# A decoder layer with a long-convolution stage and a mixture of experts: tile work moved beside the convolution and between shared expert passes

## The reference

```python
x = x + attn(layernorm(x))                       # linear attention: elu+1 feature maps, 16 heads of 32
# long convolution over the feature axis, 32 heads of 8 tokens (D_MODEL = 256 tokens, L = 512 features)
kv = einsum('bhil,bhjl->bijhl', ctx, ctx)        # products of all token pairs of a head
y  = irfft(rfft(kv, 2L) * rfft(ssm_kernel, 2L))[..., :L] + kv * D
x  = x + einsum('bijhl,bhil->bjhl', y, layernorm(x))
# mixture of experts: 16 experts, groups of 4, top 2 groups, top 4 experts, and one shared expert
w, sel = route(h @ gate_weight.T)                # h = layernorm(x), sigmoid scores
x = x + sum_e w_e * (silu(h @ G_e.T) * (h @ U_e.T)) @ D_e.T + shared(h)
```

## Time and profile before

| | us |
|---|---|
| median of 3 runs | 948.46 (948.42 to 950.93) |
| the profiled execution, its time | 946.82 |
| its span, first to last instruction | 944.0 |
| TensorE busy | 881.2 (93%) |
| VectorE busy | 592.7 (63%) |
| ScalarE busy | 377.1 (40%) |
| GpSimd busy | 385.8 (41%) |
| mean granted TensorE clock | 0.953 |

### The profile page before, as it was taken

The page is one execution under the profiler, slowest core; times in us unless marked ns, Lnnn a source line. Parts: engine busy times, 40 slices in busy tenths (PEclk is TensorE's granted clock), DMA queues, the critical chain, the costliest instruction groups (busy, mean ns, idle before and its releaser), DMA issues.

```text
span 944.0 us, 14192 instructions
## 1 busy us (share of the span) xinstructions
PE 881.2 (93%) x4356; PEld 732.3 (78%) x4356; DVE 592.7 (63%) x929; ACT 377.1 (40%) x603; POOL 385.8 (41%) x387
## 2 busy tenths in 40 slices
PE   4899999999899999967999979999999999999995
PEld 4788888888777777747987757877777777777774
DVE  5656766656479999996669964535444544444541
ACT  3323322233034433333333224556555655565552
POOL 2300000001146666653313242566565656565634
PEclk9999999999999999985569999999999999999997
DMA  9400000000026543302200145788988888888857
GB/s 330 127 1 1 1 0 0 0 0 12 23 67 203 163 110 108 108 22 74 79 34 6 67 146 170 212 217 181 210 195 201 179 206 197 200 180 196 206 112 89
DMA packets 49342, 109.39 MB, mean 116 GB/s; under 512 B 8800, under 2 KB 9312, under 8 KB 49184
## 3 DMA queue, kind: packets, MB, share of 16 engines
q0 software_dynamic: 17024, 40.48, 23.5%
q1 hardware_dynamic: 32288, 68.55, 22.1%
HBM read 78.35 MB, written 30.65 MB: 115 GB/s over the span
## 4 chain that ended last, share of the span: by engine, by line
PE 36%; DVE 7%; issue 7%; ACT 2%; POOL 1%; DMA 1%; POOLq 0%; ACTq 0%; DVEq 0%
PE PS L184 10%; PE PS L186 10%; PE PS L185 9%; PE PS L1246 3%; DVE C_rounded L1463 2%; PE PS L1184 1%; DVE y_rounded L1487 1%; PE PS L1175 1%; PE PS L1193 1%; ACT hTh L1086 1%; PE PS L1192 1%; DVE wl L1482 1%; DVE Tz_rounded L1460 1%; DMA xg<-xs_d,idx 1%; POOL xg L996 0%
## 5 line engine op out<-in xcount | busy, mean ns | idle before, releaser
L1013 POOL DMA_INDIRECT out_y<-QY,idy x72 | 119.4, 1659 | 52.7 <-ACT QY L1105 36.1
L184 PE MATMUL PS<-y_rounded,wh 128*128 128x512 f32 (+1 forms) x344 | 140.4, 408 | 0.0
L186 PE MATMUL PS<-y_rounded,wl 128*128 128x512 f32 (+1 forms) x344 | 133.9, 389 | 0.0
L185 PE MATMUL PS<-y_rounded,wh 128*128 128x512 f32 (+1 forms) x344 | 133.5, 388 | 0.0
L1497 DVE TENSOR_TENSOR hTl<-hh,hTh 128x512 fp32r<-128x512 f32 (+1 forms) x39 | 26.5, 679 | 119.4 <-ACT hTh L1086 114.5
L996 POOL DMA_INDIRECT xg<-xs_d,idx x76 | 79.0, 1040 | 34.9 <-issue 17.8
L246 POOL TENSOR_SCALAR var_eps<-mean_var 128x2 f32<-128x2 f32 x15 | 3.3, 219 | 196.2 <-DVE mean_var L357 196.2
L195 PE MATMUL PS<-qER,Tz 128*128 128x288 f32 x320 | 80.8, 407 | 1.5 <-ACT QY L318 0.8
L195 PE MATMUL PS<-prod,Tz 128*128 128x288 f32 x320 | 81.9, 412 | 0.0
L1487 DVE TENSOR_TENSOR y_rounded<-PS,y_rounded 128x512 fp32r<-128x512 f32 x76 | 50.7, 687 | 42.2 <-ACT y_rounded L1098 41.4
L186 PEld LDWEIGHTS PS<-y_rounded,wl 128*128 128x128 f32 x344 | 65.0, 189 | 14.2
(11 more groups left out here) (215 smaller groups left out, 1950.2 us busy)
## 6 DMA issues: line engine op xcount, KB each, us to landing
ws<-in_gu_w SPq DMA_DIRECT2D x38, 512.0 KB
ws<-in_dn_w SPq DMA_DIRECT2D x20, 512.0 KB, 5.3
C<-in_ctx SPq DMA_DIRECT2D x32, 256.0 KB, 2.7
Tz<-kpad_d SPq DMA_DIRECT2D x32, 256.0 KB, 3.2
xs_d<-xn SPq DMA_DIRECT2D x16, 256.0 KB, 2.0
out_y<-X SPq DMA_DIRECT2D x16, 256.0 KB
X<-in_x SPq DMA_DIRECT2D x1, 3072.0 KB, 18.7
xg<-xs_d,idx POOLq DMA_INDIRECT x76
```

The lines of the kernel that those rows point to most:

```text
L184: pe.matmul(out_, lh, rh, start=first, stop=False)
L185: pe.matmul(out_, lh, rl, start=False, stop=False)
L186: return pe.matmul(out_, ll, rh, start=False, stop=last)
L1013: nc.gpsimd.indirect_dma_start(out=out, out_offset=bass.IndirectOffsetOnAxis(ap=idy[:, t:t + 1], axis=0), in_=yo[:, t], in_offset=None, co ...
```

## The change

- Tiles are taken in another order (`tile_at`): first the eight first halves of the sequences, then the second halves. Four of them (`EARLY`) go through `t3`, addition, norm, `t4` and the split during the convolution's heads 18 to 27: their transposes write into the unused PSUM columns (`in_gaps`) behind a head's convolution. `convolve` gets a `behind` argument for that. Their router passes and stores come too; the routers run right after the last head.
- GpSimd's split of the shared weights moves from the end into heads 12 to 17, in three parts.
- The shared expert's group 0 and part of group 1 run in single steps (`shared_step`, six passes of 512 columns; `down5`) between the other twelve tiles. The down passes of all groups now come before the first slot, and the last placings lie between those of group 3; `body(0)` has no down passes.
- The counts: TensorE forms, in one PSUM bank, the count of each expert within the tile and over all tiles before it, by 16 further passes with `ones_r` over `SELr`; VectorE's running totals over tiles fall away, and those over experts become one product with a lower triangle (`lower`) and a sum.
- The one-hot matrices are formed from `free_ps`, a copy of `free` in PSUM that TensorE makes.
- VectorE's `w_lo(0, 1)` and `add_shared`, and ScalarE's `w_hi(0, 1)`, change their place around the first slots.

```diff
-def convolve(pe, i, k, chunks=range(DC)):
+def convolve(pe, i, k, chunks=range(DC), behind=None):
...
+        if behind is not None and c == DC - 1:
+            mm = behind()
...
+EARLY = SLOT_T
+ODD = CD * 2
+tile_at = [TPB * b + t for t in range(TPB) for b in range(B)]
...
+def stream_head(e):
+    return CH // 2 + 2 + 2 * e
+
+def normal_head(e):
+    return CH // 2 + 5 + 2 * e
...
+def add_to_stream(dve, n):
+    i = tile_at[n]
+    if n < EARLY:
+        h = stream_head(n)
+        dve.wait_ge(conv_ps[h % 2], DC * (h // 2 + 1))
+        dve.tensor_tensor(by_gaps(X[:, i]), by_gaps(X[:, i]), in_gaps(h % 2), ALU.add).then_inc(x2_done, 1)
+    else:
+        dve.wait_ge(t3_ps, n - EARLY + 1)
+        dve.tensor_tensor(X[:, i], X[:, i], PS[:, 4 + n % 2], ALU.add).then_inc(x2_done, 1)
+    wait_apart(dve, x2_done, n + 1)
+    dve.bn_stats(bst3[n % 4][:], X[:, i]).then_inc(bn3, 1)
+    if n >= 4:
+        wait_apart(dve, nb3s, n - 3)
+    wait_apart(dve, bn3, n + 1)
+    dve.bn_aggr(mv3[n % 4][:], bst3[n % 4][:]).then_inc(mv3s, 1)
...
+def x3_low(dve, n):
+    dve.wait_ge(xT_hi, n + 1)
+    if n < EARLY:
+        dve.tensor_tensor(low_tile(n).rearrange("p c (b n) -> p c b n", n=ODD), in_gaps(normal_head(n) % 2),
+                          high_tile(n).bitcast(F32).rearrange("p c (b n) -> p c b n", n=ODD), ALU.subtract).then_inc(xT_lo, 1)
...
+        for part in range(NG - 1):
+            pair_of_heads(6 + part)
+            shared_lo(2 * part, 2 * part + 2)
+        for e in range(EARLY):
+            pair_of_heads(stream_head(e) // 2)
+            rstd3(pool, e)
+        for i in range(stream_head(EARLY) // 2, CH // 2 - 1):
+            pair_of_heads(i)
...
+        for h in range(stream_head(0), CH):
+            head(h // 2, h % 2)
+            for e in range(EARLY):
+                if h == stream_head(e) + 2:
+                    norm(act, e)
+                if h == normal_head(e):
+                    x3_high(act, e)
...
+        for h in range(stream_head(0), CH):
+            for e in range(EARLY):
+                if h == normal_head(e):
+                    dve.wait_ge(xT_hi, e + 1)
+            terms_ahead(h // 2, h % 2)
+            for e in range(EARLY):
+                if h == stream_head(e):
+                    add_to_stream(dve, e)
+                if h == normal_head(e):
+                    x3_low(dve, e)
+            reduce((h - 1) // 2, (h - 1) % 2)
+            terms_behind(h // 2, h % 2)
...
+        for h in range(stream_head(0), CH):
+            behind = None
+            for e in range(EARLY):
+                if h == stream_head(e):
+                    behind = functools.partial(stream_back, e)
+                if h == normal_head(e):
+                    behind = functools.partial(normal_across, e)
+                if h == stream_head(e) + 2:
+                    pe.wait_ge(x2_done, e + 1)
+                if h == normal_head(e) + 2:
+                    pe.wait_ge(xT_lo, e + 1)
+            convolve(pe, h // 2, h % 2, behind=behind)
...
+        rstd3(pool, 4)
+        hidden(0, 0)
+        rstd3(pool, 5)
+        hid_lo(0, 0)
+        for n in range(6, 9):
+            rstd3(pool, n)
+        wait_apart(pool, r_in, 16 * 6)
+        nc.gpsimd.tensor_copy(tri_r[:], tri[:]).then_inc(tri_done, 1)
+        rstd3(pool, 9)
+        hidden(0, 1)
+        rstd3(pool, 10)
+        rstd3(pool, 11)
+        hid_lo(0, 1)
+        for n in range(12, NT):
+            rstd3(pool, n)
+        for g in range(1, NG):
             for c in range(IC):
                 hidden(g, c)
                 hid_lo(g, c)
-        hidden(NG - 1, 0)
...
+        for n in range(EARLY, NT):
+            if n > EARLY:
+                x3_high(act, n - 1)
+            norm(act, n)
+            if n == 5:
+                hid_hi(0, 0)
+            if n == 8:
+                silu(0, 1)
+                up(0, 1)
+            if n == 10:
+                hid_hi(0, 1)
+                act.activation(table_row[:], ident[:, 0:1], ACT.Sigmoid)
+            if n > 12:
+                y_shared_out(0, n - 13)
...
+        for n in range(EARLY):
+            router(n)
+        for d in range(DC - 1):
+            shared_step(0, 0, d)
+        t3(EARLY)
+        t3(EARLY + 1)
+        shared_step(0, 0, DC - 1)
+        steps = {4: (0, 1, 0), 5: (0, 1, 1), 6: (0, 1, 2), 7: (0, 1, 3), 9: (1, 0, 0), 10: (1, 0, 1), 11: (1, 0, 2)}
+        for n in range(EARLY, NT):
+            if n + 2 < NT:
+                t3(n + 2)
+            if n in steps:
+                shared_step(*steps[n])
+            t4(n)
+            if n > 11:
+                down5(0, n - 12)
+            if n > EARLY:
+                router(n - 1)
+        shared_step(1, 0, 3)
         router(NT - 1)
 
-        shared_gate_up(0, 0)
...
+        pe.matmul(free_ps, ident[:], free[:], start=True, stop=True).then_inc(free_ready, 1)
+        shared_gate_up(1, 1)
+        shared_gate_up(2, 0)
+        shared_down(1)
         pe.wait_ge(sel_done, 1)
-        pe.wait_ge(r_in, 16 * 6)
-        pe.wait_ge(memsets, 5)
-        sel = SEL[:].rearrange("p t e -> p (t e)")
-        pe.matmul(PS[:, 4, 0:NT * NE], tri[:], sel, start=True, stop=True)
-        pe.matmul(PS[:, 4, NT * NE:], ones[:], sel, start=True, stop=True).then_inc(count_ps, 1)
-        shared_down(0)
-        shared_gate_up(1, 1)
-        shared_gate_up(2, 0, placing=0)
-        shared_down(1, placing=SLOT_T)
-        shared_gate_up(2, 1, placing=2 * SLOT_T)
-        shared_gate_up(3, 0, placing=3 * SLOT_T)
-        shared_down(2)
-        shared_gate_up(3, 1)
+        pe.wait_ge(memsets, 6)
+        pe.wait_ge(tri_done, 1)
+        pe.matmul(PS[:, 4, 0:(NT + 1) * NE], tri_r[:], SELr[:].rearrange("p t e -> p (t e)"), start=True, stop=False)
+        for t in range(NT):
+            mm = pe.matmul(PS[:, 4, (t + 1) * NE:(NT + 1) * NE].rearrange("p (t e) -> p t e", e=NE), ones_r[:],
+                           SELr[:, t].unsqueeze(1).broadcast_to([P, NT - t, NE]), start=False, stop=(t == NT - 1))
+        mm.then_inc(count_ps, 1)
+        shared_gate_up(2, 1)
+        shared_step(3, 0, 0)
+        shared_step(3, 0, 1)
+        place(0)
+        shared_step(3, 0, 2)
+        place(1)
+        shared_step(3, 0, 3)
+        place(2)
+        for t in range(SLOT_T):
+            down5(2, t)
+            place(3 + t)
+        for d in range(DC):
+            shared_step(3, 1, d)
+            place(7 + d)
+        place(11)
+        place(12)
+        place(13)
+        down5(3, 0)
+        place(14)
+        down5(3, 1)
+        place(15)
+        down5(3, 2)
+        down5(3, 3)
...
-        link(dve.tensor_copy(TOT[:].rearrange("p t e -> p (t e)"), PS[:, 4, NT * NE:]))
-        cur, k, n = TOT, 1, 0
-        while k < NT:
-            nxt = acc[n % 2]
-            post(dve.tensor_copy(nxt[:, 0:k], cur[:, 0:k]))
-            tt(nxt[:, k:], cur[:, k:], cur[:, 0:NT - k], ALU.add)
-            cur, k, n = nxt, 2 * k, n + 1
-
-        tt(NSK[:], cur[:, NT - 1].unsqueeze(2).broadcast_to([P, NE, B * S // SLOT]),
+        tt(NSK[:], PS[:, 4, NT * NE:(NT + 1) * NE].unsqueeze(2).broadcast_to([P, NE, B * S // SLOT]),
            slotk[:].unsqueeze(1).broadcast_to([P, NE, B * S // SLOT]), ALU.is_gt)
         reduce(NS[:], NSK[:])
-        tt_post(POS[:], cur[:], TOT[:], ALU.subtract)
-        cur, k, n = NS, 1, 0
-        while k < NE:
-            nxt = se[n % 2]
-            post(dve.tensor_copy(nxt[:, 0:k], cur[:, 0:k]))
-            tt(nxt[:, k:], cur[:, k:], cur[:, 0:NE - k], ALU.add)
-            cur, k, n = nxt, 2 * k, n + 1
-        ends = cur
-        tt(base[:], ends[:], NS[:], ALU.subtract)
-        link(dve.tensor_scalar(base[:], base[:], float(SLOT), None, ALU.mult))
-
-        tt(POS[:], POS[:], base[:].unsqueeze(1).broadcast_to([P, NT, NE]), ALU.add)
-        tt(POS[:].rearrange("p t e -> p (t e)"), POS[:].rearrange("p t e -> p (t e)"), PS[:, 4, 0:NT * NE], ALU.add)
+        tt(before, lower[:], NS[:].unsqueeze(1).broadcast_to([P, NE, NE]), ALU.mult)
+        reduce(base[:], before)
+        post(dve.tensor_tensor(ends[:], base[:], NS[:], ALU.add))
+        link(dve.scalar_tensor_tensor(out=POS[:], in0=base[:].unsqueeze(1).broadcast_to([P, NT, NE]), scalar=float(SLOT),
+                                      in1=PS[:, 4, 0:NT * NE].rearrange("p (t e) -> p t e", t=NT), op0=ALU.mult, op1=ALU.add))
...
+            dve.tensor_tensor(lowhot[p], free_ps.unsqueeze(1).broadcast_to([P, TOPK, P]),
...
+                dve.tensor_scalar(colhot[p][:, r], free_ps[:, 0:NCOL], HIF[:, t, r:r + 1], TOKV[:, t, r:r + 1],
...
 
+        w_lo(0, 0)
+        w_lo(0, 1)
         add_shared(0)
-        add_shared(1)
-        w_lo(0, 0)
-        add_shared(2)
         for d in range(DC):
             x_lo(0, d)
         dve.wait_ge(es_done, 2)
         more = more_slots(dve)
         last = more + (NFULL - 1)
-        w_lo(0, 1)
+        add_shared(1)
         hidden(0, 0)
         hid_lo(0, 0)
         w_lo(0, 2)
         w_lo(1, 0)
```

(22 more changed lines are left out.)

398 lines of the change are left out of this document (215 added, 183 removed).

## The result

The changed kernel takes 940.57 us (median of 6 runs, 939.07 to 942.1), the kernel before beside it 949.04 (6 runs): the ratio is 0.9931, with a 95% interval of 0.9911 to 0.9951. It is faster by 8.5 us by the medians (6.5 by the ratio), where I forecast 16.5, and outside the 924 to 938 of the forecast's own case. The profiled execution took 940.8 us with a span of 938.9, at a mean granted clock of 0.982.

A forecast was written before the change was run, and what follows sets the result against it. Bounds taken: VectorE in the convolution, half-clock TensorE among the tiles, VectorE in the routing, then gathers. Convolution +7.8, tiles -13.6, routing -10.6, handover +0.5 sum to -15.9: span 928.1, forecast 932 us, range 918 to 950.

The forecast's parts named there:

- the forecast's own case: Whole kernel: the main outcome, a time of 924 to 938 us, given a chance of 0.55.
- R - D: Tiles, from VectorE's last convolution reduction to the last router pass: 59.6 us before, forecast 46.
- Rival 1: Tiles: the clock stays low among them, they take 77.5 us and the kernel 963, slower; chance 0.12.
- IDX to T: From the routing's list of rows to the first slot's transposes: 12.4 us forecast.
- D: Convolution: the time of VectorE's last reduction, 424.0 us before, forecast 431.8, an addition of 7.8.
- my upper bound of 9.8: Convolution: VectorE's added work for four early tiles, 2.46 us each, with nothing recovered from the collision with GpSimd's product.
- the handover: First slot's transposes to the second slot's: 17.0 us before, forecast 0.5 net longer, bounds -4 and +6.
- Rival 2: The handover eats the moved down passes' gain and half the tiles run slow: about 940 to 945 us; chance 0.17.
- (a): Routing, last router pass to the counts in VectorE: 19.9 us, 0.6 later than before, with TensorE last.
- (b): Routing, counts to the first one-hot: 10.8 us before, 6.1 forecast, a gain of 4.7.
- (c): Routing, the one-hots: 34.0 us to 32.3; stretches beside GpSimd go, reading PSUM costs 0.05 an operation.
- (d): Routing's end: list of rows 58.3 us after the last router pass by VectorE, TensorE's placings at 57.3, so VectorE last.

The follow-up runs named there:

- i: Changed kernel with VectorE's shared-row additions of three groups ahead of the first slot's low parts, the fourth's behind the hidden product; 930.5 us, ratio 0.9858.
- m: Changed kernel with GpSimd's hidden and hid_lo operations of groups 1 to 3 cut to 4-column fills, those values left out; 937.84 us, one run.
- a: Changed kernel with the second slot's remaining weight parts ahead of the third group's stores in SP's queue; 940.75 us, ratio 0.9932.
- b: Changed kernel with VectorE's additions of shared rows of groups 2 and 3 behind the first slot's second-half hidden product; 943.79 us, ratio 0.9955.
- c: Changed kernel with both the weight parts ahead of the third group's stores and the additions behind the hidden product; 944.9 us, ratio 0.9978.

## Why the prediction was right and wrong

**Right.** The kernel is faster, and by the main means forecast: the tiles at full clock. I took 46 for R - D with 41.0 as its bound at full clock, and it is 41.8; the 5 us set aside for the clock were not needed here, so this term was 4.2 too long. The early burst of 32 router passes kept full clock in this execution: they follow each other at 0.11 us from 428.19 to 431.78. That is luck in part: the fall that I expected in or behind the burst, at 2 us, came in five other executions (0.7 to 2.3 us); the 3 us among the tiles came in none that had the shared steps there. Rival 1 fell, and the run without the steps shows that it would have held without them. The Trainium skill, "TensorE: Matmul & The Clock Gate", Part 4, says that full clock does not engage for transposes. The tiles without wide passes, transposes and narrow router passes together, were granted 0.50, which fits; but at 432.20 of the kernel before the clock had risen under transposes alone, which does not, and with wide passes between the transposes it was 1.00. IDX to T, 12.4 forecast, took 11.9.

**Wrong, D: the mechanism.** I let the collision with GpSimd's product grow less once TensorE no longer set the pace, and wrote "if the collision with the product goes once their phases part". The phases did not part: I counted rstd as small work in GpSimd's idle time, and missed that it ties the start of the product behind it to VectorE's statistics. From head 15 to D the change added 12.3 us where I had 7.8; with that one step moved it added 8.2, so the step cost 4.1. This was above my upper bound of 9.8, because the bound was work added without collision added. That the products go on costing something (2.3 us, from 86.3 to 88.6) the forecast had right. The Trainium skill, "SBUF — State Buffer", Who interferes with whom, says that a VectorE operation with two SBUF inputs contends with a GpSimd instruction that reads SBUF; 0.94 against 2.01 agrees, and this rule of the Trainium skill would have pointed to `terms_behind`.

**Wrong, the handover: the size.** The prediction named all of it ("eight additions of shared rows in front of the hidden product", the stores "in front of the second slot's weights", ScalarE "up to 6 late"), gave it a bound of +6, and then took 0.5 as a net of that and of what the down passes' removal gives back. It measured +6.3. The give-back was there (17.0 to 14.9 for the second slot; 13.1 in i, which is the 4 at most). But waits in a chain of queues are not netted: each of three comes last in turn. What it did not name is the third, the scatter behind the last stores. Rival 2 had this half right and its other half, slow tiles, wrong; that its 940 to 945 holds the result is partly chance.

**Wrong, routing: small terms.** (a) 21.1 instead of 19.9: not TensorE but VectorE's single operations stretched beside GpSimd, 1.5 us by m. (b) 7.1 instead of 6.1, one more such operation (1.28 for 0.19). (c) The stretches of the one-hots went and the price was 0.06 an operation, as taken (0.05): 1.86 a tile. What was missing is the tail (d): VectorE ends its one-hots at 539.1 and the last placings, behind half-speed down passes, end 2.4 later instead of 1.0.

## What to carry to other kernels

When a small dependent step goes into an engine's queue, look at what stands behind it: it will start at a fixed distance from the step's producer, and may meet that engine's next operation every time (2.01 us for 0.94 here). When additions, stores, loads and scatters stand in order in four queues, removing one wait may only show the next, as in a, b and c; move the earliest producer (here VectorE's additions, into 8.7 us of its idle time) and leave the queues alone. Wide passes put between transposes and narrow ones can cost nothing, if the clock was low without them.

## What the runs showed of the hardware

- Mixed stretches of transposes, 32-column router passes and six 512-column passes a tile were granted 1.00; the same without the wide passes 0.50. Right after the convolution, the same program was once granted 1.00 and once 0.55 in the same 7 us, and among the eight kernels that are one program up to R five kept full clock there and three lost it for a few passes (R - D 41.7 and 42.4).
- A VectorE operation of 0.2 to 0.4 us took 0.97 to 1.40 beside GpSimd's operations on 512 columns, so a small operation can pay as much as a large one (2.01 for 0.94).
- The fp32 source in PSUM cost 0.06 us in a narrow one-input operation of 124 columns and nothing in the 512-column operation of two inputs (0.69 both ways).
- Weights moved ahead of the stores made gathers land later: the second slot's transposes waited 5.82 and 6.32 us for them in a and c, 2.56 in the changed kernel and 3.47 at most where weights and stores stood as in it.
